# Weighed values over their sums: moved from VectorE to GpSimd in two halves

## The chip, the cores and the metric

The kernel runs on one core of one Trainium2 chip. The metric is device time in microseconds (us), shorter is better. A core has five engines that run at the same time and wait for one another through semaphores: PE (TensorE, matmuls), DVE (VectorE), ACT (ScalarE), POOL (GpSimd) and SP, which here only issues DMAs. DVE and ACT read PSUM, where matmuls write; POOL works on SBUF alone.

## The reference

The program is one block of attention and two layers of a windowed transformer over 8 batches of 1024 positions with 256 channels. Only the first phase, the attention, is touched. Cut to that:

```python
q1, q2, k1, k2 = heads(x, Wq1), heads(x, Wq2), heads(x, Wk1), heads(x, Wk2)   # 16 heads of 16
v = heads(x, Wv)                                                              # 16 heads of 32
att1 = softmax(causal(q1 @ k1.T / 4))
att2 = softmax(causal(q2 @ k2.T / 4))
y = (att1 - lam * att2) @ v                  # 8 batches x 16 heads, 1024 x 32 each
yn = group_norm(y)                           # statistics over positions, per channel
out = yn @ Wc.T
x = layernorm(x + out)
```

The kernel does the division of the softmax last. For each head it sums exp(score) times values on PE, beside it exp(score) times ones (the sums), and then forms values over sums with one multiplication by the inverse of the sums. That multiplication is what the change is about.

## The kernel before, in words

The first phase walks over 128 heads g = 16 b + h (8 batches b, 16 heads h). Each engine has its own instruction stream, written out by hand, and takes it strictly in order. In iteration g of the loop:

- **PE** computes, for each of eight key blocks kb, the transposed scores of head g (`scores`, L564 helper, `ps<-kt,qt` and `ps<-qt,kt`), and the weighed values and sums of head g (`values`, L693). Between them it places 24 *pieces* of the scores of head g + 2, numbered k = 0 to 23, of which only the row maxima are wanted. The pieces alternate between two PSUM banks: a piece may only be written when the piece two places before it has been read by DVE (`pe.wait_ge(max_free, done(slot - 1))`). The piece k = 16 therefore waits until DVE has read k = 14. In most heads PE also computes a part of the projections of the next batch or of the output of the last one (`extra`, two units a head).
- **ACT** takes exp of the scores (`exps`, L1247), block by block, copies out the finished half sums (`copy_out`), and after block 1 of iteration g forms the inverse of the sums of head g - 1 in `rb` (`invert`, L1260 and L1262).
- **POOL** masks the diagonal of each block of exponentials (L2054, eight per head, the fourth block is kb = 3, the fifth kb = 4), which PE needs before it weighs the block, and prepares the scaled values (`place_values`, L2015) and the third parts of queries and keys (`low_parts`, L2005).
- **DVE** reads the 24 pieces and keeps their maxima (`piece`: L1614 for those on the diagonal, L1618 for the others). Ahead of piece 8 it does `normalise_head(g - 1)`: one `tensor_tensor` of 64 partitions by 1024 columns (L1639), `ev` times `rb` into `wy`.
- **SP** issues, in this order in iteration g, twelve DMAs with the operands of head g + 3 (L417), two with the maxima of head g + 1 (L424), and two that put the divided values of head g - 1 in place, `ya` (L435) and `yb` (L436). These wait for `wy_done`.

The values of four heads form a group. When h is a multiple of four (h = 0, 4, 8, 12, and g > 0, 31 such iterations), DVE does for the last group, right behind piece 13, `sum_group` (L1644), which adds `yb` to `ya`:

```python
def sum_group(J):
    for p in range(2):
        dve.wait_ge(y_ready[p], sent(4 * J + 4))
    dve.tensor_tensor(ya[:, J % 4, :], ya[:, J % 4, :], yb[:, :], ALU.add).then_inc(ysum_done, 1)
```

It waits for the DMAs of all four heads of the group, and the last of these is head g - 1, whose values were divided in this same iteration. Behind it, still on DVE, come piece 14, statistics of one half (L1648), piece 15, in some heads the rest of a projection (L1583), piece 16 and so on. In the iterations behind these (h = 1, 5, 9, 13) ACT and DVE turn the statistics into scales (`over_time`, L1267, L1269 and L1658 to L1664).

Below, "head 48" is iteration g = 48, and its start is the first exp of 1024 columns on ACT.

Of the kernel before, what the change touches and what calls it, by code (L numbers as in the profile page):

```python
# [8 lines left out]
ALU = mybir.AluOpType  # L9
# [34 lines left out]
def done(n):  # L44

    return n + START


def sent(n):

    return 16 * n + START
# [31 lines left out]
def slot_of(k):  # L83

    return k + (k >= T_AT)
# [49 lines left out]
def program(nc, d, nb):  # L135

    assert nb % 2 == 0
    with ExitStack() as ctx:
        top = [nc.sbuf_base]

        def sb(name, shape, dt):

            n = 2 if dt == BF16 else 4
            for x in shape[1:]:
                n *= x
            at = (top[0] + 31) // 32 * 32
            top[0] = at + n
            return nc.alloc_sbuf_tensor_at(name, shape, dt, offset=at)

        def sem(name):  # L150
            s = ctx.enter_context(nc.semaphore(name))
            counters.append(s)
            return s
# [39 lines left out]
        ev = sb("ev", [P, 1024], F32)  # L193
        wy = sb("wy", [P, 2, 1024], F32)
        rb = wy[0:64, 0, :]
# [85 lines left out]
        masked = sem("masked")  # L281
# [4 lines left out]
        rb_done = sem("rb_done")  # L286
        wy_done = sem("wy_done")
        y_ready = [sem(f"y_ready{p}") for p in range(2)]
# [89 lines left out]
        ALL = nb * HEADS  # L378
# [9 lines left out]
        def _(sp):  # L388
# [37 lines left out]

            def values_out(g):
                b, h = divmod(g, HEADS)
                sp.wait_ge(wy_done, done(g + 1))
                if h == 0 and b:  # L430
                    sp.wait_ge(out_full, done(b * 4))
                if h % 4 == 0 and g:
                    sp.wait_ge(ysum_done, done(g // 4))
                rows = slice(VC * (h % 4), VC * (h % 4 + 1))
                sp.dma_start(ya[rows, h // 4, :], wy[64:96, h % 2, :]).then_inc(y_ready[h % 2], 16)  # L435
                sp.dma_start(yb[rows, :], wy[96:128, h % 2, :]).then_inc(y_ready[h % 2], 16)  # L436
# [759 lines left out]
        def _(act):  # L1196
# [54 lines left out]
            def copy_out(g, half):  # L1251
                act.wait_ge(pv_done, done(g * 8 + 4 * half + 4))
                if half == 0:
                    act.wait_ge(wy_done, done(g))
                act.activation(ev[:, half * 512:half * 512 + 512], ps[:, 4 + half, :], ACT.Copy).then_inc(ev_done, 1)

            def invert(g):
                act.wait_ge(ev_done, done(g * 2 + 2))
                act.wait_ge(wy_done, done(g))
                act.activation(rb, ev[64:128, :], ACT.Ln).then_inc(ln_done, 1)  # L1260
                act.wait_ge(ln_done, done(g + 1))
                act.activation(rb, rb, ACT.Exp, scale=-1.0).then_inc(rb_done, 1)  # L1262
# [28 lines left out]
            for s in range(QKV_SLOTS):  # L1291
# [4 lines left out]
                else:  # L1296
                    k = s if s < 8 else s - 8
# [255 lines left out]
        def _(dve):  # L1553
# [75 lines left out]
            def copy_maxima(g, slot):  # L1629
                dve.wait_ge(max_full, done(slot + 1))  # L1630
                if g:
                    dve.wait_ge(mrow_ready, sent(2 * g))
                dve.tensor_copy(mt[:, :], psb[0:32, bank_of(slot), 0:P]).then_inc(max_free, 1)

            def normalise_head(g):
                dve.wait_ge(rb_done, done(g + 1))
                if g >= 2:
                    dve.wait_ge(y_ready[g % 2], sent(g - g % 2))
                dve.tensor_tensor(wy[64:128, g % 2, :], ev[0:64, :], rb, ALU.mult).then_inc(wy_done, 1)  # L1639

            def sum_group(J):
                for p in range(2):
                    dve.wait_ge(y_ready[p], sent(4 * J + 4))
                dve.tensor_tensor(ya[:, J % 4, :], ya[:, J % 4, :], yb[:, :], ALU.add).then_inc(ysum_done, 1)  # L1644
# [43 lines left out]
            for g in range(ALL):  # L1688
                b, h = divmod(g, HEADS)
                slot = AHEAD + g * SLOTS  # L1690
                if g + 2 < ALL:
                    for k in range(24):
                        if k == T_AT:
                            copy_maxima(g + 1, slot + k)
                        if k == 8 and g:
                            normalise_head(g - 1)
                        piece(g + 2, k, slot + slot_of(k))
                        if k == 11 and h % 4 == 1 and g > 4:
                            over_time(g // 4 - 1)
                        if k == 15:  # L1700
                            extra(g, 0)
                        if k == 17:
                            extra(g, 1)
                        if h % 4 == 0 and g:
                            if k == 13:
                                sum_group(g // 4 - 1)
                            if k == 14:
                                half_statistics(g // 4 - 1, 0)
                            if k == 16:
                                half_statistics(g // 4 - 1, 1)  # L1710
                            if k == 18:
                                statistics(g // 4 - 1)
                        if h == 4 and b and k == 17:
                            divide_z(b - 1, 0)
                        if h == 5 and b and k == 3:
                            divide_z(b - 1, 1)
                    two_parts(g + 2, slot + 24)
                elif g + 1 < ALL:
                    copy_maxima(g + 1, slot)
                    normalise_head(g - 1)  # L1720
                else:
                    normalise_head(g - 1)
            dve.wait_ge(k2_ready, done(3))
            dve.wait_ge(tab_ready, sent(2))
            for l in range(LAYERS):
# [1 line left out]
                                  tabs[1][:, :, :, :].rearrange("p w a e -> p w (a e)"),  # L1727
                                  scl[:, l, :, :].rearrange("p a e -> p (a e)").unsqueeze(1).broadcast_to([P, WIN, 4 * LD]),
                                  ALU.mult).then_inc(tab_done, 1)
            normalise_head(ALL - 1)  # L1730
            dve.wait_ge(tab_done, done(LAYERS))

            def norms(W):
# [255 lines left out]
        def _(pool):  # L1989
# [18 lines left out]
            def place_values(g):  # L2008
                b, h = divmod(g, HEADS)
                v = va[:, (g // 4) % VGROUPS, :, VC * (h % 4):VC * (h % 4 + 1)]  # L2010
                if h % 4 == 0:
                    pool.wait_ge(v_done, done(b * 8 + h // 2 + 2))
                if g >= 2:
                    pool.wait_ge(pv_done, done((g - 1) * 8))
                pool.tensor_tensor(vs[:, g % 2, :, :], v, nlam[:, h:h + 1, :].broadcast_to([P, 8, VC]),  # L2015
                                   ALU.mult).then_inc(vs_ready, 1)
# [9 lines left out]
            for k in range(8, 16):  # L2026
                low_parts(0, k)

            def window_step(kb):
                if kb == 1:  # L2030
                    for u in range(UNROLL):
                        pool.wait_ge(op_ready[u], sent(12 * ALL // UNROLL))
                    pool.memset(window[:], 0.0).then_inc(k2_ready, 1)
                    pool.memset(xs[:, :, 0:1], 0.0).then_inc(k2_ready, 1)
                if kb == 2:
                    pool.wait_ge(k2_ready, done(2))
                if 2 <= kb <= 3:
                    par = kb - 2
                    own = window[:, par, par * P:(par + 1) * P]
                    pool.affine_select(out=own, in_=own, compare_op=ALU.is_ge, fill=NEG, base=0,  # L2040
                                       pattern=[[-1, P]], channel_multiplier=1)
                if 4 <= kb <= 5:
                    par = kb - 4
                    prev = window[:, par, (1 - par) * P:(2 - par) * P]
                    i = pool.affine_select(out=prev, in_=prev, compare_op=ALU.is_ge, fill=NEG, base=0,
                                           pattern=[[1, P]], channel_multiplier=-1)
                    if kb == 5:
                        i.then_inc(k2_ready, 1)

            for g in range(ALL):  # L2050
                for kb in range(8):
                    pool.wait_ge(exp_done, done(g * 16 + 2 * kb + 2))
                    diag = probs(kb)[:, :, kb * P - first(kb):(kb + 1) * P - first(kb)]
                    pool.affine_select(out=diag, in_=diag, compare_op=ALU.is_ge, fill=0.0, base=0,  # L2054
                                       pattern=[[0, 2], [1, P]], channel_multiplier=-1).then_inc(masked, 1)
                    if kb == 1 and g + 1 < ALL:
                        place_values(g + 1)
                    if g == ALL - 2:
                        window_step(kb)
                    if kb >= 6:  # L2060
                        extra_low(g, kb - 6)
# [145 lines left out]
```

## Time and profile before

| what | value |
|---|---|
| median of 3 runs | 5799.47 us (5796.46 to 5799.69) |
| the profiled execution | 5798.98 us |
| its span | 5797.2 us |
| PE busy | 5642.3 us, 97% of the span |
| DVE, ACT, POOL busy | 71%, 60%, 17% |
| mean granted clock of PE | 0.993 of full |

```profile
span 5797.2 us, 146068 instructions
PE 5642.3 (97%) x57904; PEld 2646.8 (46%) x57904; DVE 4143.9 (71%) x10780; ACT 3455.5 (60%) x6979; POOL 960.7 (17%) x1905
PE   8999999999999999998999999999999999999998
DVE  6887888788878878786666666666666666666664
POOL 2222222222222222222000000000000101010100
PE 83%; issue 6%; ACT 6%; DVE 3%; POOL 2%; DMA 0%; POOLq 0%; ACTq 0%; SPq 0%; DVEq 0%
```

The digits cut the span into 40 equal slices and give the busy share of an engine in tenths. The first 19 slices are the first phase, which the change touches; POOL is busy there for 2 tenths. The last line shares out the chain of work that ended last: at each step what released the instruction, back from the last one.

### The profile page before, as it was taken

The numbers are of one execution on the slowest core, as the hardware profiler recorded it, in microseconds if no ns is written. First come the engines' busy times: TensorE is split into PE (matmuls) and PEld (weight loads), VectorE is DVE, ScalarE is ACT, GpSimd is POOL, SyncE is SP. The second block draws the span as 40 slices with busy tenths as digits, with TensorE's granted clock in tenths as the row PEclk, the third lists the DMA queues.
The fourth block names the chain that finished last, engine by engine and source line by source line (L and its number), as shares of the span: only waits on it lengthen the run. The fifth ranks groups of instructions, "written<-read, shape, count | busy, mean of one in ns | idle before, by whom it ended". The sixth has DMA issues, their size and how long they took to land.

```text
span 5797.2 us, 146068 instructions
## 1 busy us (share of the span) xinstructions
PE 5642.3 (97%) x57904; PEld 2646.8 (46%) x57904; DVE 4143.9 (71%) x10780; ACT 3455.5 (60%) x6979; POOL 960.7 (17%) x1905
## 2 busy tenths in 40 slices
PE   8999999999999999998999999999999999999998
PEld 3444444444444444443444444444444444444443
DVE  6887888788878878786666666666666666666664
ACT  4766666676666667665555555555555555555554
POOL 2222222222222222222000000000000101010100
PEclk9999999999999999999999999999999999999999
DMA  3333333333333333232100000000010000000000
GB/s 70 57 54 67 55 66 56 58 62 51 70 56 65 56 60 60 51 66 52 41 15 8 15 12 12 12 12 15 8 37 12 15 19 15 19 23 12 22 12 19
DMA packets 128424, 215.38 MB, mean 37 GB/s; under 512 B 39964, under 2 KB 40092, under 8 KB 126976
## 3 DMA queue, kind: packets, MB, share of 16 engines
q1 hardware_dynamic: 127744, 206.05, 17.6%
q8 instruction: 459, 7.52, 0.5%
q14 instruction: 221, 1.81, 0.1%
HBM read 45.48 MB, written 25.17 MB: 12 GB/s over the span
## 4 chain that ended last, share of the span: by engine, by line
PE 83%; issue 6%; ACT 6%; DVE 3%; POOL 2%; DMA 0%; POOLq 0%; ACTq 0%; SPq 0%; DVEq 0%
PE ps L564 22%; PE ps L693 14%; PE ps L814 12%; PE ps L996 6%; PE ps L1029 5%; PE ps L890 5%; PE ps L1016 5%; PE ps L898 4%; PE ps L915 4%; ACT pt L1247 3%; PE ps L937 2%; PE ps L866 1%; PE ps L875 1%; PE ps L948 1%; POOL pt L2054 1%
## 5 line engine op out<-in xcount | busy, mean ns | idle before, releaser
L1247 ACT ACTIVATE pt<-ps 128x1024 f32<-128x1024 f32 (+7 forms) x2048 | 1237.3, 653 | 621.4 <-PE ps L564 464.3
L693 PE MATMUL ps<-pt,va 128*32 128x512 f32 (+3 forms) x3072 | 1226.6, 487 | 19.9 <-POOL pt L2054 19.9
L693 PE MATMUL ps<-pt,ones 128*32 128x512 f32 (+3 forms) x6144 | 1236.4, 488 | 0.0
L693 PE MATMUL ps<-pt,vs 128*32 128x512 f32 (+3 forms) x3072 | 1230.1, 488 | 0.0
L1614 DVE CUSTOM_DVE_ANT_0 junk<-ps,causal 128x128 bf16<-128x128 f32 (+3 forms) x2048 | 977.9, 487 | 308.5 <-PE ps L564 292.3
L564 PE MATMUL ps<-kt,qt 96*32 96x512 bf16 (+3 forms) x12288 | 1016.6, 328 | 35.2 <-DVE mc L1614 16.3
L564 PE MATMUL ps<-qt,kt 98*32 98x512 bf16 (+3 forms) x12288 | 835.3, 328 | 22.2 <-ACT pt L1247 21.1
L1618 DVE TENSOR_REDUCE mc<-ps 128x1 f32<-128x512 f32 x1024 | 706.3, 690 | 157.6 <-PE ps L564 127.0
L2054 POOL TENSOR_SCALAR_AFFINE_SELECT pt<-pt 128x256 f32<-128x256 f32 x1024 | 469.5, 459 | 1938.2 <-ACT pt L1247 1936.7
L814 PE MATMUL ps<-wqkv,xs 128*128 128x512 f32 x1536 | 782.3, 619 | 0.0
L1364 ACT ACTIVATE sm<-sm,mxw 128x256 f32<-128x256 f32 (+1 forms) x1024 | 495.7, 485 | 339.4 <-DVE mxw L1783 339.0
L1783 DVE CUSTOM_DVE_ANT_0 sm<-ps,window 128x256 f32<-128x256 f32 (+1 forms) x1024 | 375.5, 404 | 314.5 <-PE ps L890 312.8
L564 PEld LDWEIGHTS ps<-kt,qt 96*32 96x32 bf16 x12288 | 334.5, 94 | 579.5 <-DVE mc L1618 224.7
L1372 ACT ACTIVATE ptw<-ps 128x512 f32<-128x512 f32 (+1 forms) x512 | 287.3, 561 | 450.9 <-PE ps L898 421.9
L564 PEld LDWEIGHTS ps<-qt,kt 98*32 98x32 bf16 x12288 | 322.2, 96 | 468.4 <-issue 211.6
L2067 POOL TENSOR_TENSOR nt<-rn 128x16 f32<-128x16 f32 x128 | 39.4, 308 | 2419.9 <-ACT rn L1341 2419.9
L693 PEld LDWEIGHTS ps<-pt,va 128*32 128x32 f32 x3072 | 313.4, 110 | 248.7 <-issue 36.3
L814 PEld LDWEIGHTS ps<-wqkv,xs 128*128 128x128 f32 x1536 | 256.7, 190 | 259.3 <-issue 251.7
L1016 PE MATMUL ps<-cn,w 128*114 128x512 f32 x768 | 361.5, 598 | 5.1 <-DVE hh L1861 4.3
L1029 PE MATMUL ps<-hh,w 114*128 114x512 f32 x768 | 363.5, 597 | 0.9 <-DVE hh L1861 0.9
L996 PE MATMUL ps<-cn,w 128*114 128x512 f32 x768 | 355.5, 600 | 4.4 <-ACT cn L1401 4.4
L890 PE MATMUL ps<-kp,qp 64*128 64x256 f32 (+1 forms) x2048 | 347.6, 416 | 5.8 <-DVE mxw L1783 3.7
(144 smaller groups left out, 8499.3 us busy)
## 6 DMA issues: line engine op xcount, KB each, us to landing
qt<-part SPq DMA_DIRECT2D x768, 64.0 KB, 2.4
kt<-part SPq DMA_DIRECT2D x768, 64.0 KB, 2.5
ya<-wy SPq DMA_DIRECT2D x128, 128.0 KB, 2.3
yb<-wy SPq DMA_DIRECT2D x128, 128.0 KB, 2.3
xs<-between_phases SPq DMA_DIRECT2D x32, 512.0 KB, 3.9
xt<-in_x SPq DMA_DIRECT2D x16, 512.0 KB, 5.9
between_phases<-z SPq DMA_DIRECT2D x16, 512.0 KB, 2.8
between_phases<-xo SPq DMA_DIRECT2D x16, 512.0 KB, 2.7
```

The source lines that it names most:

```text
L564: mmi = pe.matmul(ps[32 * q:32 * q + 32, bank, lo:hi], weights[:, 32 * q:32 * q + 32], moving, start=start, stop=stop)
L693: mmi = pe.matmul(ps[32 * q:32 * q + 32, 4 + half, lo - half * 512:hi - half * 512], w, probs(kb)[:, i, lo - first(kb):hi - first(kb)], st ...
L814: return pe.matmul(ps[:, bank, :], xs[:, kc, at:at + P], wqkv[l][:, kc, n * 512:n * 512 + 512], start=kc == 0, stop=kc == 1)
L890: pe.matmul(ps[:, 4 + q, 0:n], qp[rows, hp, :], kp[rows, hp, :, :].rearrange("p a k -> p (a k)")[:, 0:n], start=True, stop=True).then_inc( ...
L996: mmi = pe.matmul(ps[0:HP, fbank(6 + j), :], w1[:, kc, 1, j, :], cn[:, kc, :], start=kc == 0, stop=kc == 1)
L1016: mmi = pe.matmul(ps[0:HP, fbank(13 + j), :], w1[:, kc, 0, j, :], cn[:, kc, :], start=kc == 0, stop=kc == 1)
L1029: mmi = pe.matmul(ps[:, fbank(20 + oc), :], w2[:, j, oc * P:(oc + 1) * P], hh[:, j, :], start=j == 0, stop=j == HB - 1)
L1247: act.activation(probs(kb)[:, i, kb * P - first(kb):1024 - first(kb)], ps[:, 2 * i:2 * i + 2, :].rearrange("p a q -> p (a q)")[:, kb * P:1 ...
L1364: i = act.activation(sm[:, hp, q, 0:n], sm[:, hp, q, 0:n], ACT.Exp, scale=-1.0, bias=mxw[:, hp, q:q + 1], accum_out=sumw[:, hp, q:q + 1])
L1614: ins = dve.tensor_tensor_reduce(out=junk[:, bank - 6, 0:w], in0=ps[:, bank, 0:w], in1=causal[:, 512 - w:512], scale=1.0, scalar=NEG, op0= ...
L1618: ins = dve.reduce_max(into, ps[:, bank, 0:w], AX_X)
L2054: pool.affine_select(out=diag, in_=diag, compare_op=ALU.is_ge, fill=0.0, base=0, pattern=[[0, 2], [1, P]], channel_multiplier=-1).then_inc ...
```

## The change

The multiplication leaves DVE for POOL, for all heads but the last. It is cut into two halves of 512 columns; half 0 of head g - 1 stands behind the mask of the fourth block of head g, half 1 behind that of the fifth. Each half first waits for the mask ahead of it (its own engine) to be complete, and behind each half POOL waits for that half to be complete. Each half counts `wy_done` up by one, so those who wait for it (SP's `values_out`, ACT's `copy_out` and `invert`) now wait for twice the number. The last head stays on DVE, in two halves. Nothing else is moved: `sum_group` stays behind piece 13.

```diff
             def values_out(g):
                 b, h = divmod(g, HEADS)
-                sp.wait_ge(wy_done, done(g + 1))
+                sp.wait_ge(wy_done, done(2 * g + 2))
...
             def copy_out(g, half):
                 act.wait_ge(pv_done, done(g * 8 + 4 * half + 4))
                 if half == 0:
-                    act.wait_ge(wy_done, done(g))
+                    act.wait_ge(wy_done, done(2 * g))
...
             def invert(g):
                 act.wait_ge(ev_done, done(g * 2 + 2))
-                act.wait_ge(wy_done, done(g))
+                act.wait_ge(wy_done, done(2 * g))
...
-            def normalise_head(g):
+            def normalise_last(g):
                 dve.wait_ge(rb_done, done(g + 1))
-                if g >= 2:
-                    dve.wait_ge(y_ready[g % 2], sent(g - g % 2))
-                dve.tensor_tensor(wy[64:128, g % 2, :], ev[0:64, :], rb, ALU.mult).then_inc(wy_done, 1)
+                dve.wait_ge(y_ready[g % 2], sent(g - g % 2))
+                for half in range(2):
+                    cols = slice(half * 512, half * 512 + 512)
+                    dve.tensor_tensor(wy[64:128, g % 2, cols], ev[0:64, cols], rb[:, cols], ALU.mult).then_inc(wy_done, 1)
...
                     for k in range(24):
                         if k == T_AT:
                             copy_maxima(g + 1, slot + k)
-                        if k == 8 and g:
-                            normalise_head(g - 1)
                         piece(g + 2, k, slot + slot_of(k))
...
                 elif g + 1 < ALL:
                     copy_maxima(g + 1, slot)
-                    normalise_head(g - 1)
-                else:
-                    normalise_head(g - 1)
...
-            normalise_head(ALL - 1)
+            normalise_last(ALL - 1)
...
+            def normalise(g, half):
+                cols = slice(half * 512, half * 512 + 512)
+                pool.wait_ge(masked, done((g + 1) * 8 + half + 4))
+                if half == 0:
+                    pool.wait_ge(rb_done, done(g + 1))
+                    if g >= 2:
+                        pool.wait_ge(y_ready[g % 2], sent(g - g % 2))
+                pool.tensor_tensor(wy[64:128, g % 2, cols], ev[0:64, cols], rb[:, cols], ALU.mult).then_inc(wy_done, 1)
+                pool.wait_ge(wy_done, done(2 * g + half + 1))
...
                     if kb == 1 and g + 1 < ALL:
                         place_values(g + 1)
+                    if kb in (3, 4) and g:
+                        normalise(g - 1, kb - 3)
                     if g == ALL - 2:
                         window_step(kb)
```

## Rows read from the trace of the kernel before

**Rows 1.** Busy time by stretch: length, busy of each engine, PEclk, DMA share.

```profile
200.00:2500.00 2300.00, 2257.31 (x38723) 1034.76 (x38723) 1856.03 (x5375) 1566.92 (x2589) 606.19 (x1111) 1.00 0.33 59
```

**Rows 2.** Waits of PE, whole span: us in total, times, longest.

```profile
PE ps L564 <- ACT pt L1247: 21.1, 106, 0.5
PE ps L693 <- POOL pt L2054: 19.9, 27, 2.0
...
PE ps L564 <- DVE mc L1614: 16.3, 23, 2.6
```

**Rows 3.** Timeline of DVE, head 48: start, length, instruction.

```profile
1074.53 1.26 DVE L1639 TENSOR_TENSOR wy<-ev,wy 64x1024 f32<-64x1024 f32 x1
...
1079.28 1.22 DVE L1644 TENSOR_TENSOR ya<-ya,yb 128x1024 f32<-128x1024 f32 x1
1080.81 0.56 DVE L1614 CUSTOM_DVE_ANT_0 junk<-ps,causal 128x384 bf16<-128x384 f32 x1 [0.31 <-PE ps L564]
```

**Rows 4.** Timeline of SP, head 48.

```profile
1075.82 0.53 SPq L435 DMA_DIRECT2D ya<-wy  x1
1076.39 0.59 SPq L436 DMA_DIRECT2D yb<-wy  x1
```

**Rows 5.** Timeline of POOL, head 48: the masks of blocks 3 and 4.

```profile
1076.07 0.41 POOL L2054 TENSOR_SCALAR_AFFINE_SELECT pt<-pt 128x256 f32<-128x256 f32 x1 [1.36 <-ACT pt L1247]
1079.48 1.28 POOL L2054 TENSOR_SCALAR_AFFINE_SELECT pt<-pt 128x256 f32<-128x256 f32 x1 [3.00 <-ACT pt L1247]
```

**Rows 6.** Timeline of ACT and PE: start of heads 48 and 49, piece 16 of 48.

```profile
1066.63 1.03 ACT L1247 ACTIVATE pt<-ps 128x1024 f32<-128x1024 f32 x1
...
1086.72 1.02 ACT L1247 ACTIVATE pt<-ps 128x1024 f32<-128x1024 f32 x1 [0.18 <-PE ps L564]
...
1082.00 0.39 PE L564 MATMUL ps<-kt,qt 96*32 96x512 bf16 x4
```

**Rows 7.** By line: POOL multiplications and additions, min/median/max ns; landing of L436.

```profile
L2079 POOL TENSOR_TENSOR both<-xm x32: 1267/1270/1273, 2841.6 to 5731.3; 128x512 f32<-128x512 f32 x32
...
L2015 POOL TENSOR_TENSOR vs<-va,nlam x128: 726/734/743, 34.0 to 2678.6; 128x256 f32<-128x256 f32 x128
...
DMA to landing us min/median/max: 2.3/2.3/6.4
```

**Rows 8.** Timeline, head 56: its start, sum_group, piece 16, start of head 57.

```profile
1236.06 1.94 ACT L1247 ACTIVATE pt<-ps 128x1024 f32<-128x1024 f32 x2
...
1250.07 1.23 DVE L1644 TENSOR_TENSOR ya<-ya,yb 128x1024 f32<-128x1024 f32 x1 [1.28 <-DMA yb<-wy]
...
1251.83 0.40 PE L564 MATMUL ps<-kt,qt 96*32 96x512 bf16 x4 [0.23 <-DVE mc L1614]
...
1257.12 1.02 ACT L1247 ACTIVATE pt<-ps 128x1024 f32<-128x1024 f32 x1 [0.50 <-PE ps L564]
```

**Rows 9.** Timeline, head 45: mask of block 2 beside DVE's multiplication, then PE.

```profile
1013.68 1.22 DVE L1639 TENSOR_TENSOR wy<-ev,wy 64x1024 f32<-64x1024 f32 x1
...
1013.90 1.27 POOL L2054 TENSOR_SCALAR_AFFINE_SELECT pt<-pt 128x256 f32<-128x256 f32 x1 [2.89 <-ACT pt L1247]
...
1015.22 0.40 PE L693 MATMUL ps<-pt,va 128*32 128x256 f32 x1 [0.72 <-POOL pt L2054]
```

**Rows 10.** Starts of heads 119, 120, 121; piece 16 of head 120; stretches around it.

```profile
2540.28 1.02 ACT L1247 ACTIVATE pt<-ps 128x1024 f32<-128x1024 f32 x1 [0.64 <-PE ps L564]
...
2557.70 1.02 ACT L1247 ACTIVATE pt<-ps 128x1024 f32<-128x1024 f32 x1 [0.64 <-PE ps L564]
...
2578.82 1.02 ACT L1247 ACTIVATE pt<-ps 128x1024 f32<-128x1024 f32 x1 [0.90 <-PE ps L564]
...
2573.04 0.40 PE L564 MATMUL ps<-kt,qt 96*32 96x512 bf16 x4 [1.99 <-DVE mc L1614]
...
2571.54:2574.95 3.41, 1.32 (x24) 0.53 (x28) 3.41 (x8) 0.06 (x1) 1.11 (x1) 1.00 0.00 0
2574.95:2578.37 3.42, 3.42 (x36) 1.24 (x32) 2.03 (x8) 1.59 (x5) 0.80 (x2) 0.50 0.00 0
```

## The prediction

> **What bounds the kernel now.** I read the page first: PE is busy for 97% of the span, so the question is only where PE stands still and what the change does to that. Then the table of stretches: in the steady part of the first phase, 2300 us long, PE is busy for 2257 us, DVE for 1856 us (81%), POOL for 606 us (26%), and the granted clock is full [rows 1]. So freeing DVE of work gives nothing by itself, since DVE is not the bound; a gain can come only from the roughly 2% in which PE waits, and a loss from any new wait. The waits of PE name three releasers in this phase: ACT's exps, 0.2 us in nearly every head; a POOL mask, 27 times, 19.9 us in all; and DVE's reading of pieces, 23 times, 16.3 us [rows 2]. Last I read the timeline of one head that sums a group, engine by engine, because there the multiplication that moves has a consumer in the same iteration.
>
> Head 48 starts at 1066.63 and lasts until 1086.72, 20.09 us [rows 6]. All times below count from its start. DVE multiplies at +7.90 for 1.26 us, until +9.16 [rows 3]. SP issues `ya` at +9.19 and `yb` at +9.76 [rows 4]. The DMA lands 2.3 us behind its issue at the median, and never sooner [rows 7], so at about +12.1. `sum_group` starts at +12.65, when DVE comes to it [rows 3]; it did not wait. PE's piece 16 starts at +15.37 [rows 6].
>
> **Part 1, the multiplication goes away from DVE: a gain of 18 us, by way of the masks.** 1.26 us less on DVE, 127 times, is 160 us of DVE time, hidden by PE's own work, so I cost it at nothing. What does show is a collision. In head 45 the multiplication begins at 1013.68, and the mask of block 2 beside it takes 1.27 us, not 0.41; PE, which wants the masked block, waits 0.72 us [rows 9]. That is the wait of 27 times. One of them is the longest, 2.0 us [rows 2], and belongs to other DVE work at the end of the phase; 26 are left, 19.9 - 2.0 = 17.9 us. They go. Behind them nothing is late: the mask would be done 0.86 us sooner, and PE lost only 0.72. The stall at the end of the phase (2.0 us and what follows) comes from two long DVE multiplications; without `normalise_head` ahead of them these start some us sooner and meet other masks. I cost that at 0, between -4 and +4.
>
> The Trainium skill says of this (SBUF — State Buffer, on contention) that DVE and GpSimd share a pair of ports as an exclusive lock: a DVE instruction with two SBUF inputs and a GpSimd instruction that reads SBUF exclude each other, and whichever comes second stands for the whole length of the first. The trace agrees for the one order, with the 1.27 us above. The rule speaks against the change in the other order: two POOL instructions of 1.27 us could now hold DVE's own two-input instructions.
>
> Whether they do I take from the times of head 48. Half 0 would run from +9.9 to +11.2 and half 1 from +13.3 to +14.6 (below). DVE reads pieces in PSUM in both, up to `sum_group`; a mask beside such reading, as that of block 3, takes its usual 0.41 us [rows 5]. So 0, with an upper end of 31 times 0.5 us, 15 us, for the heads with `over_time`.
>
> **Part 2, the multiplication on POOL: its own time is hidden.** The nearest rows are an addition of 128 x 512 in the second phase, 1.27 us, and a multiplication of 128 x 256, 0.73 us [rows 7]. The new one has 512 columns, all f32, on 64 partitions. I take 1.27 us; the ends are 0.73 us (if half the partitions took half the time) and 2.5 us (if reading one half of the partitions and writing the other costs twice). The mask of block 3 starts at +9.44 and takes 0.41 us, that of block 4 would start at +12.85 [rows 5]. Half 0 fits between them with 1.7 us to spare. Half 1 ends at +14.6, about 1 us before the next mask in heads with projections. In the few heads without, that mask comes some 0.6 us later than now, and PE comes to its block later still. Queued behind these waits on POOL are only the masks. ACT's wait for `wy_done` (in `copy_out`, behind block 6) is met some 4 us ahead. Cost 0.
>
> **Part 3, the values reach `sum_group` late: a loss of 124 us.** This is the term that decides. Step by step, from the start of a head with h = 0, 4, 8 or 12:
> - mask of block 4: +12.85, and 0.41 us long, as no `sum_group` stands beside it any more (now 1.28 us, from that collision [rows 5]): +13.26;
> - hand-over 0.05 us, half 1, 1.27 us: +14.58;
> - SP issues `ya` 0.03 us behind the end and `yb` 0.57 us behind that [rows 3, 4]: +15.18. SP waits for nothing else; its next DMAs come at the end of the head;
> - landing 2.3 us later, and 0.1 us until DVE starts: `sum_group` at +17.6, against +12.65.
>
> DVE takes its stream in order, so pieces 14 and on are queued behind `sum_group`. PE may not write piece 16 before piece 14 is read. Head 56 shows the price, since there a slow DMA already made `sum_group` late: it starts at 1250.07, +14.01, after a wait of 1.28 us, and piece 16 follows 1.76 us later, at +15.77 [rows 8]. So piece 16 now comes at 17.6 + 1.76 = +19.4, against +15.37: 4.0 us in which PE stands still, as all behind it in PE's stream stands too. Head 56 also shows that nothing takes the lateness back: it lasts 21.06 us against 20.09, longer by 0.97, though piece 16 was late by only 0.40, because DVE then runs behind. I leave this second part out, because a PE at lower clock (next part) gives DVE the time to catch up. 31 heads sum a group in the loop: 31 x 4.0 = 124 us. Ends: half 1 at 0.73 us makes it 31 x 3.5 = 108; at 2.5 us, 31 x 5.2 = 162; with DVE's lag kept, 31 x 4.6 = 142.
>
> **Part 4, the granted clock falls behind these gaps: a loss of 46 us.** In head 120 PE stood still for 1.99 us ahead of piece 16, was busy for 1.32 us of the stretch that ends at 2574.95, and then had 3.41 us at half its clock, 1.2 GHz [rows 10]. Head 120 lasts 21.12 us, head 119 before it, without extra work like it, 17.42: 3.70 us more, 2.0 of them the gap, 1.7 the half clock, which is 3.41 / 2. A gap of about 3.9 us is longer, so I expect a fall in each of the 31 heads; two late heads near the end of the phase have one now, of which head 120 is one, so 29 are new. A part of a fall can lie in the gap itself, where it costs nothing, and a second stretch at half clock can follow. Ends 0 and 3.4 us; I take 1.6, near the 1.7 that was seen: 29 x 1.6 = 46 us.
>
> **The sum.** -18 + 124 + 46 = +152 us. On the profiled execution, whose 5798.98 us are 5797.2 us of span and 1.8 us around it: 5951 us. The median of the runs is 0.5 us above that execution, which changes nothing.
>
> **Rivals.**
> - *The gaps come, the clock holds.* Or the falls lie within the gaps. For it: I have a fall only beside shorter gaps. Against: shorter gaps had one. 5799 + 124 - 18 = 5905 us. Chance 0.12.
> - *Two stretches at half clock, or a much slower POOL.* For it: the gap is twice that of head 120, and the 64 to 64 partition form isn't in the trace. 5799 + 124 + 29 x 3.4 - 18 = 6004 us, and with half 1 at 2.5 us and one stretch 5989. Chance 0.12.
> - *POOL holds DVE.* By the order of the port that no row shows, 15 us more: 5966 us. Chance 0.05; it lies within the forecast's own range.
> - *Not slower.* `sum_group` finds its values in time, and only the collisions go: 5799 - 18 = 5781 us. It decides if `yb` lands before about +13.0 in the head. For it: DVE comes to `sum_group` early and has some slack, and PE is the bound. Against it: half 1 can't even start before the mask of block 4 at +12.85, and the transfer alone takes 2.3 us. Chance 0.05, of which 0.02 is for gains that come out under 0.2%.
> - The forecast itself, one fall for each gap: 0.66, with a range of its own of 5920 to 5985.
>
> About 0.2% (12 us) is what a measurement of this kernel can tell from no change. Faster 0.03, same 0.02, slower 0.95. The range runs from 5892, a little under the clock that holds, to 5995, which takes in the slow POOL and leaves out the two full stretches.
>
> **What would show it.** Right: in each fourth head DVE's L1644 has an idle time of near 5 us before it, released by the DMA of `yb`; PE's waits for DVE `mc` L1614 grow from 16 to some 130 us with 31 or more of near 4 us; heads 5 to 7 of a batch keep their 20.0 us; PE's waits for POOL masks fall to a few us; stretches of clock 0.50 stand behind the gaps. Wrong: L1644 starts before +14; the new POOL instruction is far from 1.27 us; masks of block 5 hold PE; or the gaps are there and no stretch at half clock is.

## The result and the profile after

The changed kernel takes **5943.43 us** (median of 4 runs, 5942.03 to 5944.08), against 5799.01 us for the kernel before on the same chip. The ratio is 1.025, with a 95% interval of 1.0232 to 1.0267: slower by 2.5%. The forecast was 5951 us. The profiled spans are 5942.3 and 5797.2 us, a difference of +145.1 us, which the following readings take apart.

The page after, its heads of parts 1 and 4 (the chain that ended last, by engine):

```profile
span 5942.3 us, 146450 instructions
PE 5681.9 (96%) x57904; PEld 2672.0 (45%) x57904; DVE 3987.5 (67%) x10654; ACT 3459.0 (58%) x6979; POOL 1238.6 (21%) x2159
PE   8999999999999999998799999999999999999998
POOL 2333333333333333333100000000001001010100
PE 85%; issue 6%; ACT 3%; DVE 2%; POOL 2%; DMA 1%; SPq 0%; POOLq 0%; ACTq 0%; DVEq 0%
```

DVE lost 156 us of work and POOL gained 278 us: the same multiplication costs POOL some two times as much. PE computes the same 57904 matmuls in 39.6 us more. The shares of the page look almost as before, and a reader who has only them would not find 145 us. The waits of PE name them (us in total, times, longest), against [rows 2]:

```profile
PE ps L564 <- DVE mc L1614: 143.2, 48, 6.1
PE ps L564 <- DVE mc L1618: 5.0, 9, 0.9
PE ps L693 <- POOL pt L2060: 3.2, 5, 1.8
```

The wait for DVE's reading of a diagonal piece grew from 16.3 to 143.2 us, and the wait for a POOL mask fell from 19.9 to 3.2 us. By line, `sum_group` is as long as before (min/median/max ns), but now waits for its DMA in all 31 heads; the new instruction on POOL takes 1.275 us, 254 times:

```profile
L1645 DVE TENSOR_TENSOR ya<-ya,yb x32: 1212/1226/1227, 177.5 to 2865.2; 128x1024 f32<-128x1024 f32 x32
  DMA yb<-wy: 155.0, 31
L2032 POOL TENSOR_TENSOR wy<-ev,wy x254: 1255/1275/1293, 118.1 to 2852.5; 64x512 f32<-64x512 f32 x127
```

Head 48 shows the whole path. It starts at 1118.15, and the lines are in the order of the data, from the mask of block 3 to piece 16 and the start of head 49 (start, length, instruction, wait ahead of it):

```profile
1118.15 1.02 ACT L1247 ACTIVATE pt<-ps 128x1024 f32<-128x1024 f32 x1
...
1127.60 0.41 POOL L2060 TENSOR_SCALAR_AFFINE_SELECT pt<-pt 128x256 f32<-128x256 f32 x1 [1.36 <-ACT pt L1247]
1128.09 1.28 POOL L2032 TENSOR_TENSOR wy<-ev,wy 64x512 f32<-64x512 f32 x1
...
1130.93 0.41 POOL L2060 TENSOR_SCALAR_AFFINE_SELECT pt<-pt 128x256 f32<-128x256 f32 x1 [1.56 <-ACT pt L1247]
1131.42 1.28 POOL L2032 TENSOR_TENSOR wy<-ev,wy 64x512 f32<-64x512 f32 x1
1132.73 0.53 SPq L435 DMA_DIRECT2D ya<-wy  x1
1133.30 0.59 SPq L436 DMA_DIRECT2D yb<-wy  x1
1135.70 1.22 DVE L1645 TENSOR_TENSOR ya<-ya,yb 128x1024 f32<-128x1024 f32 x1 [4.96 <-DMA yb<-wy]
1136.85 0.55 DVE L1614 CUSTOM_DVE_ANT_0 junk<-ps,causal 128x384 bf16<-128x384 f32 x1
1137.46 0.40 PE L564 MATMUL ps<-kt,qt 96*32 96x512 bf16 x4 [3.91 <-DVE mc L1614]
...
1143.63 1.94 ACT L1247 ACTIVATE pt<-ps 128x1024 f32<-128x1024 f32 x2
```

The mask of block 4 is at +12.78, half 1 at +13.27 to +14.55, the DMA of `yb` is issued at +15.15, `sum_group` starts at +17.55 and piece 16 at +19.31. Both masks take 0.41 us now, that of block 4 no longer 1.28 [rows 5], as `sum_group` no longer stands beside it. The head lasts 25.48 us, against 20.09 [rows 6]: 3.91 us of gap, and then this, in the columns of [rows 1]:

```profile
1131.97:1135.38 3.41, 1.58 (x26) 0.45 (x16) 0.00 (x0) 1.36 (x3) 1.14 (x2) 1.00 0.36 77
1135.38:1138.79 3.41, 1.33 (x24) 0.60 (x28) 3.09 (x7) 0.00 (x0) 0.00 (x0) 1.00 0.00 0
1138.79:1142.21 3.42, 3.42 (x32) 0.91 (x24) 3.23 (x8) 2.26 (x5) 0.59 (x2) 0.50 0.02 5
```

PE was busy for 1.58 and 1.33 us of two stretches, and in the next one the granted clock is 0.50, the lower level of 1.2 GHz: there 32 matmuls fill 3.42 us.

**Where the 145.1 us are**, by length of heads from first exp to first exp:

| heads | after minus before | predicted |
|---|---|---|
| h = 0, 4, 8, 12, which sum a group | +175.5 (5.66 for each of 31) | +170 |
| h = 1, 5, 9, 13, where the masks collided | -21.5 | -18 |
| h = 2, 6, 10, 14 and h = 3, 7, 11, 15 | -8.5 (0.14 each) | 0 |
| start and end of the program | -0.4 | 0 |

### The profile page after: what moved, and what is told of

The parts are those of the page before. It is cut to its first block, busy times and chain, and to the rows that moved or that the text cites. A ratio compares the mean times of both kernels' runs of the same rounds, so it can differ in the third digit from the quotient of the medians.

```text
span 5942.3 us, 146450 instructions
## 1 busy us (share of the span) xinstructions
PE 5681.9 (96%) x57904; PEld 2672.0 (45%) x57904; DVE 3987.5 (67%) x10654; ACT 3459.0 (58%) x6979; POOL 1238.6 (21%) x2159
## 4 chain that ended last, share of the span: by engine, by line
PE 85%; issue 6%; ACT 3%; DVE 2%; POOL 2%; DMA 1%; SPq 0%; POOLq 0%; ACTq 0%; DVEq 0%
PE ps L564 24%; PE ps L693 16%; PE ps L814 12%; PE ps L996 5%; PE ps L1029 5%; PE ps L890 5%; PE ps L1016 5%; PE ps L898 4%; PE ps L915 4%; PE ps L937 2%; ACT pt L1247 2%; DMA yb<-wy 1%; PE ps L866 1%; PE ps L875 1%; POOL wy L2032 1%
## 5 line engine op out<-in xcount | busy, mean ns | idle before, releaser
L693 PE MATMUL ps<-pt,ones 128*32 128x512 f32 (+3 forms) x6144 | 1264.0, 498 | 0.0
L693 PE MATMUL ps<-pt,vs 128*32 128x512 f32 (+3 forms) x3072 | 1257.8, 498 | 0.0
L693 PE MATMUL ps<-pt,va 128*32 128x512 f32 (+3 forms) x3072 | 1254.5, 497 | 3.4 <-POOL pt L2060 3.2
L1614 DVE CUSTOM_DVE_ANT_0 junk<-ps,causal 128x128 bf16<-128x128 f32 (+3 forms) x2048 | 978.3, 488 | 323.4 <-PE ps L564 306.8
L564 PE MATMUL ps<-kt,qt 96*32 96x512 bf16 (+3 forms) x12288 | 1026.0, 332 | 156.7 <-DVE mc L1614 143.2
L2060 POOL TENSOR_SCALAR_AFFINE_SELECT pt<-pt 128x256 f32<-128x256 f32 x1024 | 423.9, 414 | 1783.5 <-ACT pt L1247 1782.5
```

The lines of the kernel that those rows point to most:

```text
L564: mmi = pe.matmul(ps[32 * q:32 * q + 32, bank, lo:hi], weights[:, 32 * q:32 * q + 32], moving, start=start, stop=stop)
L693: mmi = pe.matmul(ps[32 * q:32 * q + 32, 4 + half, lo - half * 512:hi - half * 512], w, probs(kb)[:, i, lo - first(kb):hi - first(kb)], st ...
L1614: ins = dve.tensor_tensor_reduce(out=junk[:, bank - 6, 0:w], in0=ps[:, bank, 0:w], in1=causal[:, 512 - w:512], scale=1.0, scalar=NEG, op0= ...
```

## The experiments

The theory: the loss is the path from half 1 over the DMA to `sum_group` and from there to piece 16, and the fall of the clock behind that gap; where the multiplication runs matters only by when its result lands. The rival: POOL's work itself, or what it does to DVE and the masks, costs. The medians of the kernel before in these runs are 5798 to 5799 us.

**1. The multiplication whole on DVE in the heads that sum a group, on POOL in all others** (after, edited):

```diff
+                        if k == 8 and h % 4 == 0 and g:
+                            normalise_whole(g - 1)
...
-                    if kb in (3, 4) and g:
+                    if kb in (3, 4) and g and g % 4:
```

> In the 31 iterations that sum a group (h = 0, 4, 8, 12) the multiplication is whole on DVE again, ahead of piece 8; in all others it stays on POOL in two halves. Theory (the whole loss is the late arrival at sum_group and the clock behind it): those 31 heads last as before (20.1, 20.5), all others as in the changed kernel, which took 21.5 us off the heads with h = 1, 5, 9, 13 and 8.5 us off the rest: 5799 - 30 = 5769 us, no stretch at half clock every fourth head. Rival (POOL's multiplications cost something by themselves, by the port or by later masks): over 5785 us.

Measured: 5768.18 us (5766.06 to 5772.28), ratio to before 0.9948 (0.9934 to 0.9961). This beats both kernels. Its waits of PE and, below, the wait of `sum_group` for its DMA:

```profile
PE ps L564 <- DVE mc L1614: 16.0, 23, 2.6
PE ps L693 <- POOL pt L2068: 3.3, 5, 1.8
...
  DMA yb<-wy: 8.5, 9
```

The wait for DVE is back at 16 us, and the collisions stay away. POOL still does 96 of the 127 multiplications, at no cost, so the rival falls. Against before, the 31 heads with a sum change by +1.2 us in all, those behind them by -18.5, the other two kinds by -4.0 and -4.3.

**2. The sum later, the multiplication as it is** (after, with `sum_group` behind piece 18 and the statistics behind pieces 19, 21 and 22, not 13, 14, 16 and 18):

```diff
-                            if k == 13:
+                            if k == 18:
```

> The changed kernel, all multiplications on POOL as there, but sum_group stands behind piece 18 on DVE and not behind 13 (the statistics behind 19, 21 and 22). The values land at +17.5 and DVE comes to sum_group at about +18.1. Theory (only the place of the waiting consumer makes the loss): PE isn't held at piece 16, the clock does not fall; 2.8 us of DVE work come late in the head and may hold PE by up to 1 us in the 31 heads: 5769 to 5800 us. Rival (POOL's instructions or the later DMA cost PE by themselves): above 5850 us.

Measured: 5804.29 us (5801.02 to 5808.79), ratio 1.0013 (1.0004 to 1.0022). With all of the multiplication still on POOL, 139 of the 144 us are gone: the late consumer was the loss. The range is missed by 4 us. The 31 heads with a sum are 19.7 us shorter than before in all, but the heads behind them 37.5 us longer: the statistics end later than before, and in head 57, for one, PE waits for DVE 0.5 and 0.4 us within its first 2 us. In six of these heads a stretch at half clock follows, and these six make 17 of the 37.5 us. A part of it comes from `sum_group` itself, here by line, and in its timeline in head 48, where POOL is beside it:

```profile
L1645 DVE TENSOR_TENSOR ya<-ya,yb x32: 1214/1463/1955, 177.0 to 2727.1; 128x1024 f32<-128x1024 f32 x32
...
1091.06 1.16 POOL L2001 TENSOR_TENSOR part<-rest,part 128x512 bf16<-128x512 f32 x1
1091.34 1.96 DVE L1645 TENSOR_TENSOR ya<-ya,yb 128x1024 f32<-128x1024 f32 x1 [0.56 <-DMA yb<-wy]
1092.17 1.39 POOL L2060 TENSOR_SCALAR_AFFINE_SELECT pt<-pt 128x256 f32<-128x256 f32 x1
```

POOL's addition was there first, and `sum_group` took 1.96 us for its 1.22; the mask that came while `sum_group` ran took 1.39 for its 0.41. So the collision goes in both orders. Behind heads 24, 72 and 92, where `sum_group` took 1.22 us, the next head is 0.4 us longer than before; where it took 1.47 us, mostly 0.6. The Trainium skill (SBUF — State Buffer, Who interferes with whom) has it so: an instruction of DVE with two SBUF inputs and one of GpSimd that reads SBUF exclude each other. This trace agrees in kind: 0.74 us more, a little less than the 0.88 us that POOL's addition had left.

**3. Both halves one block earlier** (after, halves behind the masks of the third and fourth blocks):

```diff
-                    if kb in (3, 4) and g:
-                        normalise(g - 1, kb - 3)
+                    if kb in (2, 3) and g:
+                        normalise(g - 1, kb - 2)
```

> Both halves stand one key block earlier on POOL (behind the masks of the third and fourth block). yb lands some 3.4 us sooner, sum_group starts at about +14.1 in its head. By head 56 of the kernel before (start of sum_group at +14.01, head longer by 0.97 us, no fall of the clock) the 31 heads cost 1.0 us each, and 30 us are gained elsewhere: 5799 + 31 - 30 = 5800 us. Rival (any wait there makes the clock fall too, 1.6 us a head): 5850 us.

**4. Half 1 one block later** (after, halves behind the masks of the fourth and sixth blocks):

```diff
-                    if kb in (3, 4) and g:
-                        normalise(g - 1, kb - 3)
+                    if kb in (3, 5) and g:
+                        normalise(g - 1, (kb - 3) // 2)
```

> Half 1 stands behind the mask of the sixth block, not the fifth. It ends at about +17.15, sum_group starts at +20.15, 2.6 us later than in the changed kernel. Theory: PE stands still for 6.5 us ahead of piece 16; 31 x 2.6 = 81 us: 6024 us, and up to 50 us more where a second stretch at half clock follows. Rival (something else than the arrival sets the start of piece 16): well under 6000 us.

Measured: number 3 took 5819.78 us, ratio 1.0033 (1.0021 to 1.0046); number 4, from a single run, 6028.41 us. Head 48 of number 3 (it starts at 1073.38), and then of number 4 (1148.95):

```profile
1087.67 1.23 DVE L1645 TENSOR_TENSOR ya<-ya,yb 128x1024 f32<-128x1024 f32 x1 [1.71 <-DMA yb<-wy]
1089.43 0.40 PE L564 MATMUL ps<-kt,qt 96*32 96x512 bf16 x4 [0.66 <-DVE mc L1614]
```

```profile
1169.03 1.23 DVE L1645 TENSOR_TENSOR ya<-ya,yb 128x1024 f32<-128x1024 f32 x1 [7.49 <-DMA yb<-wy]
1170.79 0.62 PE L564 MATMUL ps<-kt,qt 96*32 96x512 bf16 x4 [6.44 <-DVE mc L1614]
```

`sum_group` starts at +14.29 and +20.08, with +17.55 between them; piece 16 follows each time 1.76 us behind, as in [rows 8], and the gap is 0.66, 3.91 and 6.44 us. So the loss follows the time at which half 1 is done, block by block, with the same amount of work on POOL. Number 4 came within 5 us of its expectation. Number 3 took 20 us more than expected: 22 of the 31 heads have no stretch at half clock, and head 48, one of them, is 1.25 us longer than before, for a `sum_group` 1.64 us later. But in some of the 31 the DMA landed later (`sum_group` up to +16.05), and 9 of the 31 have half clock, against 3 before. The 31 heads lost 50.3 us in all, 1.6 each. I had priced every head at 1.0, by head 56 of the kernel before.

**5. The gap filled** (after; in 21 of the 31 heads, those with h = 0, 8 and 12 outside the last batch's 8 and 12, PE repeats four groups of a projection into a free PSUM bank, unused, ahead of piece 16):

```diff
+                if g % 4 == 0:
+                    filler(g, 4)
```

> The changed kernel, with four extra matmul groups of 0.86 us each on PE ahead of piece 16 in those sum heads that have a projection there (h = 0, 8, 12, 21 heads); they repeat the first part of it, so nothing of the result changes. Theory (a half clock follows from PE's idle gap and costs 1.6 us a head beside it): the gap of 3.9 us shrinks to about 0.5, sum_group starts at +17.55 still, the 21 heads last 23.9 us and not 25.5, the eight heads with h = 4 keep 27.0: 5943 - 34 = 5909 us. Rival (the time beyond the gap is DVE running late, not the clock): no change or slower, 5943 us or more, although the gap is filled.

Measured: 5917.25 us, ratio 1.0205 (1.0191 to 1.0219). Head 48, start 1106.33, and the stretch around piece 16:

```profile
1120.69 4.46 PE L564 MATMUL ps<-xt,wqk 128*32 128x512 f32 x40
1123.88 1.23 DVE L1658 TENSOR_TENSOR ya<-ya,yb 128x1024 f32<-128x1024 f32 x1 [4.96 <-DMA yb<-wy]
1125.64 0.40 PE L564 MATMUL ps<-kt,qt 96*32 96x512 bf16 x4 [0.48 <-DVE mc L1627]
...
1119.00:1126.00 7.00, 6.52 (x76) 1.97 (x72) 2.12 (x4) 1.36 (x3) 2.10 (x3) 1.00 0.18 40
```

`sum_group` is still at +17.55 and piece 16 at +19.31: here the filler makes nothing later or sooner. But PE is busy, the clock stays full in all 21 filled heads, and head 48 takes 24.60 us, not 25.48. Head 56 (h = 8) went from 26.61 to 24.56, head 108 (h = 12) from 25.59 to 23.98, while head 36 (h = 4, not filled) kept its half clock and took 27.42 us, against 27.04 in the changed kernel. So filling gave back 0.9, 2.0 and 1.6 us in these three, and 25.2 us in all 21, 1.2 a head. This is the least that the clock cost there, as late transfers and DVE's lag take a part back, and it is a cost of its own beside the gap. The miss of 8 us is not settled: in some heads the transfers landed later than in the changed kernel (`sum_group` at +18.2 to +18.75), and with the clock full DVE's lag shows in a second gap of 0.55 us.

**6. The multiplication in two halves on DVE, nothing on POOL** (before, edited). After the heads h = 2 and 3 of each group had come out 0.14 us shorter without a wait in the view of waits that explained it, I compared where each piece starts in head 46. DVE's work ahead of piece 10 and that piece, before (start 1026.60), and then after (start 1078.42):

```profile
1034.50 1.26 DVE L1639 TENSOR_TENSOR wy<-ev,wy 64x1024 f32<-64x1024 f32 x1
1035.79 0.69 DVE L1618 TENSOR_REDUCE mc<-ps 128x1 f32<-128x512 f32 x1
1036.54 0.40 PE L564 MATMUL ps<-kt,qt 96*32 96x512 bf16 x4
```

```profile
1086.71 0.69 DVE L1618 TENSOR_REDUCE mc<-ps 128x1 f32<-128x512 f32 x1 [0.43 <-PE ps L564]
1088.22 0.39 PE L564 MATMUL ps<-kt,qt 96*32 96x512 bf16 x4
```

Before, the multiplication makes DVE read piece 8 until +9.88, and piece 10 starts at +9.94, right behind it; after, piece 8 is read by +8.98 and piece 10 starts at +9.80, when PE comes to it. PE waited 0.14 us, but the modelled ends of its matmuls overlap, so the view shows no idle time. Half a multiplication ahead of piece 8 should then be enough:

```diff
-                        if k == 8 and g:
-                            normalise_head(g - 1)
+                        if k in (8, 9) and g:
+                            normalise_half(g - 1, k - 8)
```

> The kernel before, with the multiplication on DVE cut in two: 512 columns ahead of piece 8, 512 ahead of piece 9. Theory (in the plain heads of before, PE lost 0.14 us at piece 10 because piece 8 was read 1.26 us late, hidden in the waits view by the overlap of matmuls): plain heads go from 20.01 to 19.87 us, as they did in the changed kernel, 13 us in all; the mask of block 2 is held for a half only, 10 us more of the 18; values 0.6 us later in the sum heads, up to 5 us back: 5781 us. Rival (the 0.14 us come from POOL or ACT): 5788 us or more and plain heads still 20.01.

**7. Number 1 with those halves on DVE** in its heads with a sum, in place of the whole.

> As the version with DVE in the 31 sum heads and POOL in the others (5768 us), but with DVE's multiplication cut in two, ahead of pieces 8 and 9. Theory: 0.14 us less in each of 31 heads, 4 us, against values that come 0.6 us later where a DMA is slow, up to 5 us: 5764 to 5770 us.

Measured: number 6 took 5804.75 us, ratio 1.0013 (1.0004 to 1.0022), and number 7 took 5781.79 us, 0.9973 (0.9963 to 0.9983): both miss. Head 46 of number 6 (start 1028.61):

```profile
1036.51 0.73 DVE L1647 TENSOR_TENSOR wy<-ev,wy 64x512 f32<-64x512 f32 x1
1037.25 0.69 DVE L1618 TENSOR_REDUCE mc<-ps 128x1 f32<-128x512 f32 x1
1037.97 0.69 DVE L1647 TENSOR_TENSOR wy<-ev,wy 64x512 f32<-64x512 f32 x1
1038.06 0.88 POOL L2064 TENSOR_SCALAR_AFFINE_SELECT pt<-pt 128x256 f32<-128x256 f32 x1 [1.36 <-ACT pt L1247]
1038.41 0.39 PE L564 MATMUL ps<-kt,qt 96*32 96x512 bf16 x4
```

Piece 10 is at +9.80, as the reading of the 0.14 us says. But the second half starts at +9.36, where the mask of block 3 runs: that mask takes 0.88 us for its 0.41, and piece 9 is read later. Step by step against before, PE is 0.13 us early at piece 10, even again at the values behind that mask (+10.38), and 0.10 us late from piece 11 on. The heads h = 2 and 3 are 0.11 us longer than before. And the values are ready 0.7 us later, so the 31 heads with a sum lose 13.4 us (number 6) and 13.0 us (number 7), by the same path as the changed kernel: `sum_group` waits for its DMA 21.1 and 20.7 us, 31 times each, against 7.0 us and 8 times before. I had looked at the piece, not at the mask and the consumer.

**8. Numbers 3 and 2 joined, by less** (halves behind the third and fourth masks, `sum_group` behind piece 15, statistics behind 16, 17 and 19).

> All multiplications on POOL, behind the masks of the third and fourth block (values land at about +14.2), and sum_group behind piece 15, where DVE comes at about +15.0, the statistics behind 16, 17 and 19. Theory: nobody waits, and a slow DMA has more slack than before; all heads as in the changed kernel outside the 31, and these some 0.1 us under the kernel before: 5764 us. Rival (masks of the fourth block come late behind a POOL half): 5775 us and more, with PE waits on POOL masks.

Measured: 5781.23 us (5776.87 to 5789.08), ratio 0.9973 (0.9963 to 0.9983). All of the multiplication is on POOL and the kernel is a little faster than before, but 17 us over the expectation. The DMA is no longer the reason, and a DVE piece is (the wait of `sum_group`, then of PE):

```profile
  DMA yb<-wy: 4.4, 8
...
PE ps L564 <- DVE mc L1618: 39.4, 45, 1.6
```

PE's waits for POOL masks are 2.4 us, so the expectation's rival is not it either. The sum and its statistics now stand closer to the end of the head, and pieces behind them are read late: 34 of the 39.4 us lie in the 31 heads with a sum. Number 1, which leaves `sum_group` where it was, stays the best.

## Why the prediction was right

The sign, the place and the mechanism held. The size held too (+152 against +145.1 us), but with some luck: part 1 missed a gain of 12 us, and in part 4 the count of stretches and the price of each were both off, in opposite ways.

- **Part 1, the collisions: -18 predicted, -16.7 measured** in PE's waits for masks. The end of the phase came out within 1 us, and `sum_group` was not held by POOL in the changed kernel (1227 ns at most). Number 2 shows that it is at another place.
- **Part 1 was too small, in two ways.** "Freeing DVE of work gives nothing by itself" was wrong by 0.14 us a head, 8.5 us in the heads with h = 2, 3, 6, 7 and so on. And "PE lost only 0.72" behind a held mask was wrong too: in head 49 PE is 0.87 us earlier from the values behind that mask on, which is the mask's whole 0.86 us, so these heads gave 21.5 us and not 18. The bound was right (PE), but PE's hidden waits stand in no view of waits. Together 12 us more gain than forecast; the heads with a sum, 5.5 us over their 170, took a part back, and what is left is nearly the 7 us by which the sum was too high.
- **Part 2, the half on POOL: 1.27 us predicted, 1.275 measured**, the same as an instruction with 128 partitions [rows 7], and hidden, as numbers 1 and 8 show.
- **Part 3, `sum_group` at +17.6 and piece 16 at +19.4: measured +17.55 and +19.31.** 124 us predicted; in the 31 heads PE's wait for L1614 grew by 126.9 us and its other waits fell by 5.6, so 121.4 us net. Numbers 3 and 4 move the cause by a block either way, and gap and time follow.
- **Part 4, the clock: 46 us predicted, 54.1 us left over**: 175.5 us less the 121.4 us of waits, 1.75 a head, which is the clock with whatever DVE's lag adds. The price of a single stretch was right: in head 48 one stretch with PE busy throughout costs 3.41 / 2 = 1.7 us. The count was not. The 31 heads hold 48 stretches at half clock against 3 before, in heads 4, 120 and 124: 45 new ones, where the prediction had 29, one for each gap. In the heads with h = 0 and 12 it is mostly one, in those with h = 4 and 8 mostly two. A second one costs less than 1.7 us more, because the first then begins while PE still stands still, as here in head 56, where piece 16 comes at 1317.44:

```profile
1316.29:1319.70 3.41, 2.26 (x16) 0.66 (x20) 3.41 (x8) 0.47 (x1) 0.00 (x0) 0.50 0.00 0
1319.70:1323.11 3.41, 3.41 (x36) 1.15 (x32) 2.18 (x7) 1.71 (x5) 0.24 (x1) 0.50 0.00 0
```

So 29 stretches at 1.6 us stand in the sum for 45 at some 1.2, and that these two products are near each other is luck. What decides between one and two stretches stays open.

- **DVE's lag, left out: rightly so for this kernel.** With the clock kept full (number 5) it is there, as 0.55 us.

## What to carry to other kernels

Before a step is moved to a later place, look for its consumer in the same iteration, and count what is queued behind that consumer: here values that were ready 5.4 us later (+14.55, not +9.16) cost 5.7 us in each such head, and sparing only the iterations that have the consumer turned 2.5% slower into 0.5% faster. A gap of about 4 us on PE cost more than itself here, because the clock fell with it: about 1.4 times the gap. Compare the lengths of like iterations as well as the waits: a wait of 0.1 to 0.2 us behind overlapping matmuls was in no view of waits here, and over the phase it made some 12 us.

## What was not expected of the hardware

- DVE can be held by POOL as POOL by DVE: a 128 x 1024 addition of 1.22 us took up to 1.96 us beside POOL's addition, which reads SBUF (number 2).
- POOL takes 1.275 us for 64 x 512 and 1.27 us for 128 x 512 [rows 7]: half the partitions save nothing, and the multiplication as a whole costs 2.55 us, against 1.26 on DVE.
- Beside a DVE multiplication of 0.69 us a mask of 0.41 us takes 0.88, beside one of 1.22 us it takes 1.27 [rows 9].
